# Row maxima of the second query chunk: the causal mask added by VectorE inside the maximum, in place of a masking product on TensorE

## The chip, the cores and the metric

The kernel runs on one core of a Trainium2 chip. The metric is the device time of one execution in microseconds (us). The kernel before took 1107.32 us (median of 3 runs, 1106.44 to 1109.43).

## The reference

Four sequences of 1024 rows of 256 numbers go through a linear attention (layer norm, three projections, no softmax), and then through a block with causal softmax attention (16 query heads, 4 key/value heads, 16 numbers a head) and a mixture of experts (8 experts, the top 2 for each row). What the change touches is the softmax:

```
scores = jnp.einsum('bqhd,bkhd->bhqk', q, k) * scale
causal = jnp.tril(jnp.ones((S, S), dtype=bool))
scores = jnp.where(causal[None, None], scores, jnp.finfo(scores.dtype).min)
probs = jax.nn.softmax(scores, axis=-1)
attn = jnp.einsum('bhqk,bkhd->bqhd', probs, v).reshape(B, S, NH * HD)
x = x + jnp.einsum('bso,ho->bsh', attn, wo)
```

The softmax subtracts each query row's maximum over the keys it may see. That maximum is what is computed in another way.

## The kernel before

All work is cut into steps with names ("max", "score", "pv", "wo", ...). A planner, `plan()`, runs before the program is built: it holds a price for each step on each engine (`work_of`, L159 to L183, and the table above it), plays all steps against each other, and writes out a fixed order for each engine. The program then follows these orders, and semaphores carry every dependency. So a changed price or a changed dependency in the planner moves instructions that the change does not name.

Per batch there are a projection part, four head groups (one key/value head and its four query heads) of attention, and a closing part. The head groups of one batch overlap with the projections of the next, and later with expert blocks. After the last head group only expert blocks are left.

A head group works in two query chunks of 512 rows (`r` is 0 or 1). For each chunk three things happen:

- **Row maxima** ("max", L1902 to L1921 on TensorE, L1715 to L1724 on VectorE). TensorE lays query rows on the PSUM partitions and keys on the columns: 128 query rows of a head against all keys that they may see. In the second chunk (r = 1) one unit is one head and one block jj of 128 query rows: a product over the first 512 keys (L1914) into one bank, and one over the w = 128, 256, 384 or 512 keys of the own chunk (L1919) into the next bank. The last 128 of these columns lie on the diagonal: there a third product (L1920, identity times a triangle of -1e38) adds the mask. VectorE then takes the maximum over all 512 + w columns (L1724) into one column of `mx`. There are 16 such units in a second chunk, and 16 head groups, so 256 units. In the first chunk the units take 2 or 4 heads at once (L1917, L1919, L1920; 96 VectorE instructions in all).
- The maxima are transposed (L1925), split and negated (L1731, L1733), and sent by SyncE into two extra rows of the stacked queries (L984), so that the score product itself subtracts them.
- **Scores and values** ("score" L1932, exponential on ScalarE L1267, mask of the probabilities on GpSimd L1121, "pv" L1946). The result leaves through ScalarE (L1274) into `heads_out`, and SyncE "packs" it into `attnT` (L995, L998).

A "max" unit of the second chunk takes two of the seven PSUM banks that all steps share. They come free when L1724 has finished. The planner also holds back a TensorE step whose follower on VectorE would have more than 1.7 us of work ahead of it.

At the end of a batch, "wo" multiplies `attnT` with the output weights (L1953), VectorE adds the residual (L1746), and "square_sum" on ScalarE (L1220) squares each row for the next norm; the squares themselves go to a scratch tile `squares`, only their sum is used. Each waits for the one before it, as both write that tile. The pack of the next batch waits until the last "wo" has read `attnT` (L996).

Where the planner sees TensorE idle it puts in dummy products ("warm", L1826).

Of the kernel before, what the change touches and what calls it, by code (L numbers as in the profile page):

```python
# [9 lines left out]
BF16 = mybir.dt.bfloat16  # L10
I32 = mybir.dt.int32
U32 = mybir.dt.uint32
ALU = mybir.AluOpType
ACT = mybir.ActivationFunctionType
AX = mybir.AxisListType

P = 128
NBATCH, SEQ, D = 4, 1024, 256
KD = D // P
TPB = SEQ // P  # L20
# [138 lines left out]
def work_of(step):  # L159
    stage, *at = step  # L160
    if stage == "gram":
        took = ("PE", 0.865 * TPB / gram_steps(at[0]))
        return (took, ("ACT", 0.49)) if at[1] == gram_steps(at[0]) - 1 else (took,)
    if stage == "split":
        b, c, u, i = at
        return ((("DVE", 0.6) if not b else ("POOL", 1.22), ("ACT", 0.53), ("POOL", 1.13), ("ACT", 0.53), ("DVE", 0.6) if not b else ("POOL", 1.13))[i],)
    if stage == "max":
        b, g, r, u = at
        jj, h0, nh, pitch, w = max_units(r)[u]
        columns = CH + w if r else nh * w  # L170
        return ("PE", (columns + P * nh) / 2400 + 0.01), ("DVE", 0.07 + columns / 960)
    if stage in ("score", "pv"):
        b, g, r, kt = at[:4]
        w = CH - max(kt * P - r * CH, 0)
        if stage == "score":
            n = heads_in(r, kt)[0]
            return ("PE", n * w / 2400 + 0.01), ("ACT", 0.06 + n * w / 1200)
        last = kt == KEYS[r][-1]
        return (("PE", 0.23 + w / 600), ("ACT", 0.49)) if last else (("PE", 0.23 + w / 600),)
    if stage == "up":  # L180
        took = 1.72 if at[0] < STAGED else 1.82
        return (("PE", took), ("DVE", 0.6)) if at[1] else (("PE", took), ("ACT", 0.49), ("DVE", 0.6))
    return WORK_OF[stage]  # L183
# [15 lines left out]
def plan():  # L199
# [39 lines left out]
    def needs(step):  # L239
# [79 lines left out]
            packed = [("pack", *chunk_at(m - 2))] if at[3] == last_kt[at[2]] and m > 1 else []  # L319
            return [scored, ("v", b, 1)] + before + packed  # L320
        if stage == "pack":
            closed = [("wo", b - 1, TPB - 1)] if b else []
            i = b * KD + at[1] // 2 - 1
            return [("pv", *at, last_kt[at[2]])] + closed + [("recip_store", i // KD, i % KD)] * (i >= 0)
        if stage == "recip":
# [342 lines left out]
def mega_kernel(nc, x, wtheta, wphi, wgT, ln1, ln2, wqkvT, wo, woT, gateT, w13T, w2T,  # L668
                rope_q, rope_k, eye, tri, ids, out):
    with ExitStack() as ctx:  # L670
# [5 lines left out]
        def sb(name, shape, dt=F32):  # L676
            return ctx.enter_context(nc.sbuf_tensor(name, shape, dt))[:]
# [9 lines left out]
        def grid(view, a):  # L687
            return view.rearrange("p (a b) -> p a b", a=a)
# [44 lines left out]
        ln2_s = sb("ln2_s", [P, KD])  # L733
        ident = sb("ident", [P, P])
        identb = sb("identb", [P, P], BF16)
        causal = sb("causal", [P, P], BF16)
        before = sb("before", [P, P], BF16)
        onesb = sb("onesb", [P, P], BF16)

        st = sb("st", [P, 2 * TPB * 6]).rearrange("p (s t c) -> p s t c", s=2, t=TPB)  # L740
        mv = sb("mv", [P, 2 * TPB * 2]).rearrange("p (s t c) -> p s t c", s=2, t=TPB)
        sumsq = sb("sumsq", [P, TPB])
        squares = sb("squares", [P, D], BF16)
        rt = sb("rt", [P, 3 * 6 * TPB]).rearrange("p (s a t) -> p s a t", s=3, a=6)

        scales, shifts = (sb(n, [P, NBATCH * 2 * TPB]).rearrange("p (b a t) -> p b a t", b=NBATCH, a=2) for n in ("scales", "shifts"))
# [44 lines left out]
        route_mem = sb("route_mem", [P, sum(route_sizes)])  # L791
        assert max(NB) * (NE - 1) <= 4 * n8
        routing = [carve(route_mem, route_sizes)] * len(GROUPS)

        def hot(gi):
            return routing[gi][4].bitcast(BF16)[:, 0:len(GROUPS[gi]) * TPB * NE]
# [108 lines left out]
        def _(e):  # L905
# [37 lines left out]
            for step in orders["SP"]:  # L943
# [42 lines left out]
                elif stage == "pack":  # L986
# [6 lines left out]
                    q.wait_ge(*slot("pack", 2, m - 2, NPACK))  # L993
                    landed(q, "recips_store", 2, b * KD + g // 2)
                    e.dma_start(sums[part * 32:(part + 1) * 32, :], heads_out[m % 2][HD:P:32, :]).then_inc(sem[f"pack{m % 2}"], 16)  # L995
                    q.wait_ge("wo_mm", TPB * b)  # L996
                    for hh in range(GRP):
                        e.dma_start(attnT[row + hh * HD:row + (hh + 1) * HD, k, r * CH:(r + 1) * CH], heads_out[m % 2][32 * hh:32 * hh + HD, :]  # L998
                                    ).then_inc(sem[f"pack{m % 2}"], 16)
# [171 lines left out]
        def _(e):  # L1171
            q = Queue(e, sem)
            for step in orders["ACT"]:
# [39 lines left out]
                elif stage == "square_sum":  # L1213
# [2 lines left out]

                    q.wait_ge("norm3", NORM3_STEPS * (b - 1) + 1)

                    q.wait_ge("square_sum", nth[step] - 1)
                    e.activation(squares, hrow[:, j, 0:D], ACT.Square, accum_out=sumsq[:, j:j + 1]).then_inc(sem["square_sum"], 1)  # L1220
                elif stage == "xnT":
                    b, c = at
                    q.wait_ge("xnT_mm", nth[step])
# [85 lines left out]
        def _(e):  # L1309
# [322 lines left out]
            for step in orders["DVE"]:  # L1632
                stage, *at = step
                if stage == "prepare":
# [3 lines left out]
                    e.tensor_scalar(causal, tri_in[:, 0:P], MASKED, None, ALU.mult).then_inc(sem["const"], 1)  # L1638
                    e.tensor_copy(before, tri_in[:, P:2 * P]).then_inc(sem["const"], 1)
                    e.memset(onesb, 1.0).then_inc(sem["const"], 1)  # L1640

                    e.memset(pv_bank, 0.0).then_inc(sem["const"], 1)
                    q.wait_ge("load_wqkv", 32)
# [71 lines left out]
                elif stage == "max":  # L1715
# [1 line left out]
                    jj, h0, nh, pitch, w = max_units(r)[u]  # L1717
                    to = mx[:, r, :].rearrange("p (h j) -> p h j", h=GRP)[:, h0:h0 + nh, jj]
                    took = turn[step][0]
                    took = took[:, 0:CH + w].unsqueeze(1) if r else took[:, 0:nh * pitch].rearrange("p (h k) -> p h k", h=nh)[:, :, 0:w]  # L1720
                    q.wait_ge("max_mm", nth[step])

                    q.wait_ge("maxT_mm", chunk(b, g, r) - 1)
                    e.tensor_reduce(to, took, AX.X, ALU.max).then_inc(sem["max"], 1)  # L1724
                elif stage == "maxT":
                    b, g, r = at
                    m, bk = chunk(b, g, r), turn[step][0]
# [87 lines left out]
        def _(e):  # L1815
            q = Queue(e, sem)
            offset = {}
            for step in orders["PE"]:
# [83 lines left out]
                elif stage == "max":  # L1902
# [8 lines left out]
                    for c in range(nh):  # L1911
                        rows_of = s[0:STACK, r, h0 + c, jj * P:(jj + 1) * P]
                        if r:
                            e.matmul(bk[:, 0:CH], rows_of, s[0:STACK, 0, GRP, :], start=True, stop=True)  # L1914
                        to = bk[:, CH:CH + w] if r else bk[:, c * pitch:c * pitch + w]
                        if w == P and not r:
                            m = e.matmul(to, rows_of, s[0:STACK, r, GRP, 0:w], start=False, stop=c == nh - 1)  # L1917
                        else:
                            e.matmul(to, rows_of, s[0:STACK, r, GRP, 0:w], start=True, stop=False)  # L1919
                            m = e.matmul(to[:, w - P:w], identb, causal, start=False, stop=True)  # L1920
# [126 lines left out]
```

## Time and profile before

| | |
|---|---|
| median of 3 runs | 1107.32 us |
| profiled execution, its own time | 1107.03 us |
| its span, first to last instruction | 1105.3 us |
| TensorE busy | 1063.3 us, 96% |
| VectorE busy | 742.3 us, 67% |
| ScalarE busy | 569.6 us, 52% |
| mean granted clock of TensorE | 0.992 |

A matmul's row covers its way through the array, so rows of matmuls overlap, and 96% busy does not mean that the array takes in columns 96% of the time: what one product costs is the distance from its start to the start of the next. The chain of waits is followed back from the last instruction, at each step to what released it; an engine's share of it says where the time of the run was decided.

### The profile page before, as it was taken

How to read it: one execution, taken by the hardware profiler on the slowest of the kernel's cores; microseconds unless marked ns; L12 is line 12 of the kernel's file. 1: busy time of each engine (PE TensorE's matmuls, PEld its weight loads, DVE VectorE, ACT ScalarE, POOL GpSimd, SP SyncE). 2: the span in 40 equal slices, each digit the busy share in tenths (PEclk: the TensorE clock that was granted, in tenths of full speed). 3: DMA queues.
4: the chain of work that ended last, by engine and by line, in shares of the span. 5: the costliest groups of instructions: out<-in, count | busy, mean ns of one | idle time of the engine just before them, and what ended most of it. 6: DMA issues, size and time to landing. Idle time of an engine off the chain costs nothing.

```text
span 1105.3 us, 20176 instructions
## 1 busy us (share of the span) xinstructions
PE 1063.3 (96%) x6972; PEld 660.7 (60%) x6972; DVE 742.3 (67%) x1530; ACT 569.6 (52%) x1106; POOL 407.8 (37%) x476
## 2 busy tenths in 40 slices
PE   7999999999998999899899999999999999999997
PEld 6766454564444333343344444446668999999996
DVE  4699997677677777669977689624484555555552
ACT  3564557646666788657466665663332222222220
POOL 1020413715532143331244532455547633333332
PEclk9999999999999899899999999999999999999999
DMA  6335121322225466542253340223344433222221
GB/s 189 122 101 153 38 79 57 94 73 82 85 75 149 152 194 209 150 142 79 66 138 96 86 139 25 52 68 84 96 92 105 97 49 49 46 45 45 47 42 11
DMA packets 85989, 102.32 MB, mean 93 GB/s; under 512 B 17121, under 2 KB 73569, under 8 KB 85889
## 3 DMA queue, kind: packets, MB, share of 16 engines
q1 hardware_dynamic: 71584, 81.39, 25.5%
q0 software_dynamic: 14304, 19.63, 9.5%
q8 instruction: 58, 0.95, 0.4%
q14 instruction: 43, 0.34, 0.1%
HBM read 56.15 MB, written 41.01 MB: 88 GB/s over the span
## 4 chain that ended last, share of the span: by engine, by line
PE 70%; DVE 20%; issue 3%; ACT 3%; DMA 2%; POOL 1%; SPq 1%; POOLq 0%; DVEq 0%
PE psum L1986 15%; PE psum L2002 11%; DVE mx L1724 10%; PE psum L1946 9%; PE psum L1978 7%; PE psum L1932 7%; PE psum L1919 3%; PE psum L1914 3%; PE psum L1953 3%; PE psum L1900 3%; ACT probs_mem L1267 2%; PE psum L1966 1%; PE psum L1845 1%; PE psum L1920 1%; PE psum L1993 1%
## 5 line engine op out<-in xcount | busy, mean ns | idle before, releaser
L1724 DVE TENSOR_REDUCE mx<-psum 128x1 f32<-128x640 f32 (+6 forms) x352 | 347.4, 1023 | 70.7 <-PE psum L1920 67.4
L1267 ACT ACTIVATE probs_mem<-psum 128x512 f32<-128x512 f32 (+1 forms) x608 | 308.1, 585 | 167.6 <-PE psum L1932 166.4
L1121 POOL TENSOR_SCALAR_AFFINE_SELECT probs_mem<-probs_mem 128x512 f32<-128x512 f32 x128 | 82.7, 647 | 304.7 <-ACT probs_mem L1267 304.5
L1166 POOL DMA_INDIRECT out<-yout,labels x71 | 112.0, 1577 | 208.7 <-DVE yout L1802 140.7
L1932 PE MATMUL psum<-stack_mem 98*128 98x512 bf16 (+3 forms) x768 | 173.2, 329 | 7.9 <-DVE mx L1724 4.0
L1946 PE MATMUL psum<-probs_mem,v 128*17 128x512 f32 (+3 forms) x1536 | 161.9, 497 | 2.6 <-POOL probs_mem L1121 1.4
L1919 PE MATMUL psum<-stack_mem 96*128 96x256 bf16 (+3 forms) x448 | 126.0, 313 | 0.1
L1932 PEld LDWEIGHTS psum<-stack_mem 98*128 98x128 bf16 x768 | 64.1, 98 | 90.3 <-DVE mx L1724 25.9
L1914 PE MATMUL psum<-stack_mem 96*128 96x512 bf16 x256 | 98.3, 388 | 8.8 <-DVE mx L1724 7.1
L1978 PE MATMUL psum<-w_mem,blockT 128*128 x200 | 95.2, 598 | 2.2 <-issue 1.6
L1920 PE MATMUL psum<-causal,identb 128*128 128x128 bf16 x448 | 96.6, 221 | 0.0
L2002 PE MATMUL psum<-w_mem,gatedT 128*128 x384 | 91.4, 381 | 0.2 <-ACT probs_mem L1267 0.2
L1986 PE MATMUL psum<-blockT,probs_mem 128*128 128x128 f32 x736 | 89.6, 275 | 0.0
L1986 PE MATMUL psum<-blockT,stack_mem 128*128 128x128 f32 x736 | 89.5, 275 | 0.0
L1986 PEld LDWEIGHTS psum<-blockT,probs_mem 128*128 128x128 f32 x736 | 87.6, 192 | 1.2
L1986 PEld LDWEIGHTS psum<-blockT,stack_mem 128*128 128x128 f32 x736 | 87.5, 192 | 1.2
L1291 ACT ACTIVATE gated<-psum 128x512 f32<-128x512 f32 x48 | 28.7, 597 | 105.9 <-PE psum L1978 57.5
L2002 PEld LDWEIGHTS psum<-w_mem,gatedT 128*128 128x128 f32 x384 | 70.6, 190 | 16.6 <-issue 8.7
L1786 DVE COPY blockT<-psum 128x256 f32<-128x256 f32 x71 | 29.9, 421 | 74.2 <-PE psum L1966 74.2
L1151 POOL DMA_INDIRECT routed<-hrow,route_mem x64 | 63.6, 994 | 20.1 <-issue 12.1
L1914 PEld LDWEIGHTS psum<-stack_mem 96*128 96x128 bf16 x256 | 24.9, 97 | 69.6 <-DVE mx L1724 37.6
L1946 PEld LDWEIGHTS psum<-probs_mem,v 128*17 128x17 f32 x1536 | 26.5, 95 | 66.1 <-issue 44.0
(209 smaller groups left out, 1509.3 us busy)
## 6 DMA issues: line engine op xcount, KB each, us to landing
block<-routed SPq DMA_DIRECT2D x71, 129.0 KB, 2.1
w_mem<-in_w13T SPq DMA_DIRECT2D x16, 512.0 KB, 5.6
qk_parts<-w_mem SPq DMA_DIRECT2D x16, 384.0 KB, 2.5
stack_mem<-qk_parts SPq DMA_DIRECT2D x32, 192.0 KB, 3.3
w_mem<-in_x SPq DMA_DIRECT2D x8, 512.0 KB, 5.3
out<-w_mem SPq DMA_DIRECT2D x8, 512.0 KB, 3.8
x_late<-out SPq DMA_DIRECT2D x8, 512.0 KB, 4.9
stack_mem<-qk_parts SPq DMA_DIRECT2D x32, 128.0 KB, 2.8
```

The source lines that it names most:

```text
L1121: e.affine_select(pb[:, :, q0:q0 + P], pb[:, :, q0:q0 + P], [[0, GRP], [1, P]], ALU.is_ge, 0.0, base=0, channel_multiplier=-1).then_inc(se ...
L1166: e.indirect_dma_start(out_rows, bass.IndirectOffsetOnAxis(ap=labels[w % NLABEL].bitcast(I32)[:, 0:1], axis=0), youts[w % NYOUT], None, bo ...
L1267: e.activation(probs[m % 2][:, hh:hh + n, q0:CH], grid(turn[step][0][:, 0:n * (CH - q0)], n), ACT.Exp, scale=float(HD) ** -0.5).then_inc(s ...
L1724: e.tensor_reduce(to, took, AX.X, ALU.max).then_inc(sem["max"], 1)
L1914: e.matmul(bk[:, 0:CH], rows_of, s[0:STACK, 0, GRP, :], start=True, stop=True)
L1919: e.matmul(to, rows_of, s[0:STACK, r, GRP, 0:w], start=True, stop=False)
L1920: m = e.matmul(to[:, w - P:w], identb, causal, start=False, stop=True)
L1932: m = e.matmul(bk[:, i * (CH - q0):(i + 1) * (CH - q0)], s[0:STACK + NMAX, kt // TPR, GRP, kt % TPR * P:(kt % TPR + 1) * P], s[0:STACK + N ...
L1946: m = e.matmul(pv_bank[32 * hh:32 * hh + HD + 1, q0:CH], v1[:, b, kt, g, :], pb[:, hh, q0:CH], start=(kt == KEYS[r][0]), stop=(kt == KEYS[ ...
L1978: m = e.matmul(bk, blockT[w % 2][:, k], w13_s[:, k, bass.ds(offset[w] + half * FFN, FFN)], start=(k == 0), stop=(k == KD - 1))
L1986: m = e.matmul(bk[:, c * P:(c + 1) * P], slots[w % NSLOT][:, k, half * FFN + c * P:half * FFN + (c + 1) * P], blockT[w % 2][:, k], start=( ...
L2002: m = e.matmul(bk[:, 0:D], rowsT[:, k * P:(k + 1) * P], w2_mem[:, bass.ds(offset[w] + k * D, D)], start=(k == 0), stop=(k == KF - 1))
```

## The change

The second chunk's masking product goes, and the maximum on VectorE becomes an instruction with two inputs that adds the mask, writes the sum back over the scores in PSUM, and keeps the maximum. The mask comes from a new tile: 512 columns of zeros, and behind them the triangle that `causal` was. The 512 + w columns are read as two rows of n = (512 + w) / 2; the pattern over the mask tile starts its two rows 128 columns apart, so that the first falls on zeros alone and the second ends in the triangle. The first chunk keeps its masking products and its plain maxima.

Besides this: `squares` is given up and L1220 writes its squares into the part of `attnT` that the "wo" before it has read, without waiting for its forerunner; the pack of the next batch therefore waits for the last "square_sum" in place of the last "wo"; the planner's price of a "max" unit of the second chunk loses 128 columns on TensorE and stays as it was on VectorE; one memset is added at the start.

```diff
-        return ("PE", (columns + P * nh) / 2400 + 0.01), ("DVE", 0.07 + columns / 960)
+        return ("PE", (columns + P * nh * (not r)) / 2400 + 0.01), ("DVE", 0.07 + columns / 960)
...
-            closed = [("wo", b - 1, TPB - 1)] if b else []
+            closed = [("square_sum", b - 1, TPB - 1)] if b else []
...
-        causal = sb("causal", [P, P], BF16)
+        masking = sb("masking", [P, CH + P], BF16)
+        causal = masking[:, CH:]
...
-        squares = sb("squares", [P, D], BF16)
...
+        def masked(w):
+            n = (CH + w) // 2
+            return bass.AP(masking.tensor, masking.offset + CH - (n - P) - P, [masking.ap[0], [P, 2], [1, n]])
...
-                    q.wait_ge("wo_mm", TPB * b)
+                    q.wait_ge("square_sum", TPB * b)
...
-                    q.wait_ge("square_sum", nth[step] - 1)
-                    e.activation(squares, hrow[:, j, 0:D], ACT.Square, accum_out=sumsq[:, j:j + 1]).then_inc(sem["square_sum"], 1)
+                    e.activation(attnT.bitcast(BF16)[:, 0, j * D:(j + 1) * D], hrow[:, j, 0:D], ACT.Square, accum_out=sumsq[:, j:j + 1]).then_inc(sem["square_sum"], 1)
...
+                    e.memset(masking[:, 0:CH], 0.0).then_inc(sem["const"], 1)
...
-                    e.tensor_reduce(to, took, AX.X, ALU.max).then_inc(sem["max"], 1)
+                    if r:
+                        q.wait_ge("const", 6)
+                        keys = grid(turn[step][0][:, 0:CH + w], 2)
+                        e.tensor_tensor_reduce(keys, keys, masked(w), 1.0, -3e38, ALU.add, ALU.max, to).then_inc(sem["max"], 1)
+                    else:
+                        e.tensor_reduce(to, took, AX.X, ALU.max).then_inc(sem["max"], 1)
...
-                        if w == P and not r:
+                        if r:
+                            m = e.matmul(to, rows_of, s[0:STACK, r, GRP, 0:w], start=True, stop=True)
+                        elif w == P:
                             m = e.matmul(to, rows_of, s[0:STACK, r, GRP, 0:w], start=False, stop=c == nh - 1)
```

On TensorE, early in the second chunk of the first head group, the program before has three products for each unit (L1914 the first 512 keys, L1919 the own keys, L1920 the mask), with scores (L1932) and values (L1946) between:

```order
L1914 MATMUL psum<-stack_mem 128x512
L1919 MATMUL psum<-stack_mem 128x256
L1920 MATMUL psum<-causal,identb 128x128
L1932 MATMUL psum<-stack_mem 128x384
L1914 MATMUL psum<-stack_mem 128x512
L1919 MATMUL psum<-stack_mem 128x256
L1920 MATMUL psum<-causal,identb 128x128
L1932 MATMUL psum<-stack_mem 128x384 x2
L1946 MATMUL psum<-probs_mem,v 17x512 x4
```

and the changed one, at the same place (L1926 is the old L1914, L1929 the own keys, L1946 the scores, L1960 the values):

```order
L1926 MATMUL psum<-stack_mem 128x512
L1929 MATMUL psum<-stack_mem 128x256
L1946 MATMUL psum<-stack_mem 128x384 x2
L1926 MATMUL psum<-stack_mem 128x512
L1929 MATMUL psum<-stack_mem 128x256
L1946 MATMUL psum<-stack_mem 128x384
L1960 MATMUL psum<-probs_mem,v 17x512 x4
```

The masking product is gone, and a score product has changed place with a unit, since the planner's times have shifted. Such exchanges go through the rest of the order. TensorE issues 5042 matrix instructions and loads of offsets where it issued 5290: 256 masking products fewer, 8 dummy products more (59 in place of 51).

On VectorE, at the start of the second chunk of the head group that meets the close of the first batch, the order before has single maxima with the short steps of a reciprocal root between them:

```order
L1383 TENSOR_SCALAR rt<-sumsq 128x8
L1724 TENSOR_REDUCE mx<-psum 128x1
L1322 TENSOR_SCALAR rt<-rt 128x8
L1724 TENSOR_REDUCE mx<-psum 128x1
L1325 TENSOR_SCALAR rstd<-rt 128x8
```

The changed order there:

```order
L1734 ISA psum,mx<-psum,masking 128x640
L1734 ISA mx 128x1
L1389 TENSOR_SCALAR rt<-sumsq 128x8
L1734 ISA psum,mx<-psum,masking 128x640
L1734 ISA mx 128x1
L1328 TENSOR_SCALAR rt<-rt 128x8
L1734 ISA psum,mx<-psum,masking 128x640
L1734 ISA mx 128x1
L1331 TENSOR_SCALAR rstd<-rt 128x8
```

Each maximum has become two instructions: one that adds, writes back and keeps the maximum, and a second with no tensor input that writes one column of `mx`. There are 256 such pairs. The short steps have moved behind one maximum that stood after them.

On SyncE, where the first packs of the second batch follow the close of the first (L984 the maxima, L995 and L998 the pack, L1022 and L1039 stores and weight loads), the order before is:

```order
L1039 DMA w_mem<-in_w13T 128x1024
L995 DMA sums<-heads_out 32x1x64
L998 DMA attnT<-heads_out 16x512 x4
L1022 DMA out<-x_late 128x256
L995 DMA sums<-heads_out 32x1x64
L998 DMA attnT<-heads_out 16x512 x4
L984 DMA stack_mem<-mneg_parts 1x16x128 x2
```

and the changed one (L990 the maxima, L1001 and L1005 the pack, L1029 the store):

```order
L1029 DMA out<-x_late 128x256
L990 DMA stack_mem<-mneg_parts 1x16x128 x2
L1029 DMA out<-x_late 128x256
L1001 DMA sums<-heads_out 32x1x64
L1005 DMA attnT<-heads_out 16x512 x4
L1001 DMA sums<-heads_out 32x1x64
L1005 DMA attnT<-heads_out 16x512 x4
```

The maxima now go out ahead of the first pack, and not behind the second.

## Rows read from the trace of the kernel before

**Rows 1.** The page: busy time of each engine; all maxima, busy, mean ns | idle before, releaser.
```profile
PE 1063.3 (96%) x6972; PEld 660.7 (60%) x6972; DVE 742.3 (67%) x1530; ACT 569.6 (52%) x1106; POOL 407.8 (37%) x476
...
L1724 DVE TENSOR_REDUCE mx<-psum 128x1 f32<-128x640 f32 (+6 forms) x352 | 347.4, 1023 | 70.7 <-PE psum L1920 67.4
```
**Rows 2.** Busy time in three stretches; columns as the second line says.
```profile
core 0: us, PE busy (x) PEld busy (x) DVE busy (x) ACT busy (x) POOL busy (x), PEclk, DMA share, GB/s
0.00:70.00 70.00, 60.74 (x318) 48.66 (x318) 46.82 (x204) 33.04 (x66) 9.70 (x22) 1.00 0.48 142
70.00:705.00 635.00, 609.67 (x4100) 284.92 (x4099) 500.23 (x945) 406.34 (x832) 224.09 (x266) 0.99 0.36 106
705.00:1105.00 400.00, 392.89 (x2557) 327.09 (x2556) 195.27 (x382) 130.24 (x209) 174.02 (x189) 1.00 0.32 63
```
**Rows 3.** Chain of waits, 70 to 705 us, by line: shares of the stretch.
```profile
by line: DVE mx L1724 18.1%; PE psum L1946 13.4%; PE psum L1932 10.2%; PE psum L1919 5.9%; PE psum L1914 5.6%; issue 4.3%; PE psum L1900 4.1%; PE psum L1953 3.9%; ACT probs_mem L1267 3.0%; PE psum L1978 2.6%; PE psum L1920 2.2%; DMA block<-
```
**Rows 4.** The line L1724: its forms, who waited for it (us, times).
```profile
L1724 DVE TENSOR_REDUCE mx<-psum x352: 669/1006/1227, 75.9 to 702.8; 128x1 f32<-128x640 f32 x32, 128x1 f32<-128x768 f32 x32, 128x1 f32<-128x896 f32 x32, 128x1 f32<-128x1024 f32 x32
...
  PEld psum L1914: 39.3, 65
  PEld psum L1932: 25.9, 40
  PEld psum L1925: 8.4, 18
```
**Rows 5.** Groups by shape, VectorE: busy, mean ns | idle before, releaser.
```profile
L1724 DVE TENSOR_REDUCE mx<-psum 128x1 f32<-128x1024 f32 x64 | 75.7, 1218 | 19.0 <-PE psum L1920 18.7
L1724 DVE TENSOR_REDUCE mx<-psum 128x1 f32<-128x896 f32 x64 | 67.2, 1083 | 14.2 <-PE psum L1920 13.9
L1724 DVE TENSOR_REDUCE mx<-psum 128x1 f32<-128x768 f32 x64 | 59.8, 951 | 15.5 <-PE psum L1920 15.5
L1724 DVE TENSOR_REDUCE mx<-psum 128x1 f32<-128x640 f32 x64 | 50.0, 810 | 1.2 <-PE psum L1920 0.8
L1724 DVE TENSOR_REDUCE mx<-psum 128x4 f32<-128x512 f32 x16 | 11.0, 687 | 2.3 <-PE psum L1917 2.3
L1668 DVE TENSOR_TENSOR w_mem<-psum,w_mem 128x512 f32<-128x512 f32 x16 | 11.0, 686 | 9.1 <-PE psum L1867 9.0
```
**Rows 6.** TensorE in order of time: start us, us.
```profile
348.45 0.27 PE L1919 MATMUL psum<-stack_mem 96*128 96x256 bf16 x1
348.56 0.22 PE L1920 MATMUL psum<-causal,identb 128*128 128x128 bf16 x1
348.62 0.38 PE L1914 MATMUL psum<-stack_mem 96*128 96x512 bf16 x1
```
**Rows 7.** VectorE in order of time, short steps between maxima.
```profile
345.75 0.81 DVE L1724 TENSOR_REDUCE mx<-psum 128x1 f32<-128x640 f32 x1
346.48 0.15 DVE L1322 TENSOR_SCALAR rt<-rt 128x8 int32<-128x8 int32 x1
346.55 0.81 DVE L1724 TENSOR_REDUCE mx<-psum 128x1 f32<-128x640 f32 x1
```
**Rows 8.** ScalarE in order of time: a sum of squares and its second instruction.
```profile
339.60 0.42 ACT L1220 ACTIVATE squares<-hrow 128x256 bf16<-128x256 f32 x1 [1.00 <-DVE hrow L1746]
339.93 0.19 ACT L1220 ACTIVATION_READ_ACCUMULATOR squares<-hrow 128x1 f32 x1
340.02 1.13 ACT L1212 ACTIVATE w_mem<-w_mem,ln_s 128x1024 f32<-128x1024 f32 x1
```
**Rows 9.** The last square of the first batch, and the pack behind it on SyncE.
```profile
344.61 0.41 ACT L1220 ACTIVATE squares<-hrow 128x256 bf16<-128x256 f32 x1
344.92 0.19 ACT L1220 ACTIVATION_READ_ACCUMULATOR squares<-hrow 128x1 f32 x1
...
344.46 2.44 SPq L998 DMA_DIRECT2D attnT<-heads_out  x4
```
**Rows 10.** VectorE's write into PSUM at the start.
```profile
L1642 DVE MEMSET psum<- 128x512 f32 x1 | 0.5, 485 | 0.1
```

More of the change, by code:

```diff
@@ L1719, in _ @@
                     took = turn[step][0]
-                    took = took[:, 0:CH + w].unsqueeze(1) if r else took[:, 0:nh * pitch].rearrange("p (h k) -> p h k", h=nh)[:, :, 0:w]
+                    took = took[:, 0:nh * pitch].rearrange("p (h k) -> p h k", h=nh)[:, :, 0:w]
                     q.wait_ge("max_mm", nth[step])
                     q.wait_ge("maxT_mm", chunk(b, g, r) - 1)
-                    e.tensor_reduce(to, took, AX.X, ALU.max).then_inc(sem["max"], 1)
+                    if r:
[4 more added lines that the diff above has]
+                        e.tensor_reduce(to, took, AX.X, ALU.max).then_inc(sem["max"], 1)
                 elif stage == "maxT":
```

## The prediction

> **What bounds the kernel now.** I read the page first. TensorE is busy 96% of the span, VectorE 67%, ScalarE 52% [rows 1]; so TensorE is the first suspect, but a matmul's row covers its way through the array, and says little about idle time. Second, the three stretches [rows 2]. All 352 maxima run between 76 and 703 us [rows 4], so only the stretch of 70 to 705 us can be touched. There VectorE is busy 500.2 of 635 us, 79%, and TensorE 609.7; in the 400 us of expert blocks behind it VectorE has half its time free and nothing of the change runs. Third, the chain of waits inside the stretch [rows 3]. The reader is to see two owners. The maxima L1724 alone hold 18.1% of it, more than any line of TensorE; the TensorE lines that the row names hold 47.9% together. So neither engine bounds the stretch alone: where the ring of PSUM banks is full, TensorE waits for a maximum; elsewhere VectorE waits for TensorE. Fourth, who waits at L1724 [rows 4]: VectorE sat idle 67.4 us before it until L1920 was done [rows 1], and in the other direction TensorE's weight loads waited 39.3, 25.9 and 8.4 us for L1724, in 123 waits. The waits go both ways. A microsecond saved on TensorE and one added on VectorE both count in part, and the question is which part.
>
> **The change, part by part.**
>
> *Removed on TensorE.* 256 masking products. Their row says 0.22 us, but the next product starts 0.06 us later, and the 256 columns of L1919 before it took 0.11 us from start to start, so 128 columns are 0.055 us [rows 6]. The clock there is the full one, and its mean in the stretch is 0.99 [rows 2]. 256 x 0.055 = 14.1 us of the array's time. That is one end: TensorE bound everywhere. For the other I take the chain: L1920 has 2.2% of 635 us = 14.0 us of it [rows 3], over 448 products, of which 256 go (352 maxima, of which 96 are the first chunk's, and L1920 stands 192 times there): 14.0 x 256/448 = 8.0 us. I take 9 us, near the chain's figure, since some of the 4.3% that the chain calls issue lies before such products. The range keeps 8 and 14, and zero for the case that the planner fills the room badly.
>
> *The maximum with the addition.* The same number of columns, but two inputs, a write of every column back into PSUM, and another reduction. No row of before shows this instruction. Rows next to it: a plain maximum over 512 columns takes 687 ns, and a two-input addition with one input in PSUM that writes 512 columns takes 686 [rows 5]. So a second input and a full output cost nothing against a maximum. A write into PSUM of 512 columns takes 485 ns [rows 10], less than either. The per-column part is (1218 - 810) / 384 = 1.06 ns [rows 5]. I take the first instruction at the old duration. Bounds: 0 below (I see no way in which two inputs are quicker than one), and above, a second pass per column, which is a rival below.
>
> *Added on VectorE: a second instruction.* The changed order has, behind each of the 256, an instruction without tensor input that writes one column of `mx`. The nearest relatives are the short steps of the reciprocal root. They last 0.15 us, but between two maxima they cost less: the short step starts 0.73 us after the maximum's start, before its 0.81 are over, and the next maximum follows 0.07 us later [rows 7]. ScalarE has the very pair already: its second instruction lasts 0.19 us and the next one starts 0.09 us after it [rows 8]. So a price of 0.07 to 0.09 us, and I take 0.08. The lower bound is 0.07. The upper: if nothing overlaps, 0.15 for the second instruction, plus the 0.08 (0.81 - 0.73) by which the maximum's end is now hidden, 0.23 us. At 0.08 it is 256 x 0.08 = 20.5 us of VectorE's time, which goes to 520.7 us. What of it is on the path? L1724 has 18.1% of 635 = 114.9 us of the chain, and 347.4 us of busy time [rows 1]: 33%. 20.5 x 0.33 = 6.8 us. The signal that frees the two banks comes with the second instruction, and is later by the same step, which this share already holds.
>
> The Trainium skill (VectorE: DVE Perf Modes, section Two Vector instructions with no wait between them) says that an operation which also writes its accumulator out is two instructions; the order of the changed program agrees.
>
> *The planner.* Its TensorE price for a unit falls by 128 columns, its VectorE price is not raised for the second instruction. It therefore believes VectorE 256 x 0.08 us quicker than I do, and holds TensorE back too late. The orders exchange score products and units throughout, and put 8 dummy products more. I cannot price that from rows; I take 0 with 4 us either way.
>
> *The squares.* The wait for the forerunner goes: the sixth square of the batch starts at 339.60 us and the eighth at 344.61 [rows 8, 9], 2.5 us apart each, so nothing was waiting there. The pack of the next batch now waits for the last square. In before it issued at 344.46 us, and the last square and its sum end at 344.92 + 0.19 = 345.11 [rows 9]: 0.65 us later, on SyncE, with the next maxima's transfer and the stack loads queued behind it. The changed order puts one transfer of maxima ahead of this pack, which takes what hurts most out of the queue. I cost it at 0, at most 0.7 for each of three batches. The added memset of 512 columns (485 ns, [rows 10]) falls in the first 70 us, where VectorE is free a third of the time [rows 2]: 0, or 0.5 if that cover is not there.
>
> **The sum.** -9 + 6.8 = -2.2 us. The profiled execution took 1107.03 us, so 1104.8 us; it stands 0.3 us under the median of the runs, which I let pass. Taking the balance the other way round: the change breaks even where the pair costs 9 / (256 x 0.33) = 0.107 us more than the single maximum.
>
> **The rivals.**
>
> *TensorE decides nearly everywhere.* For: it is at 96%, and what VectorE loses falls into its own idle time (70.7 us before L1724, [rows 1]). Then 14.1 us are gained and the short price of 0.07 is charged at half its share: 256 x 0.07 x 0.17 = 3 us. -11 us, 1096 us. Against: 123 waits of weight loads for L1724.
>
> *The pair does not overlap, and VectorE becomes the bound: slower.* Each unit costs 0.23 us more, VectorE is busy 500.2 + 58.9 = 559 us of the stretch, 88%. At today's share 58.9 x 0.33 = 19.5 us, less 8 us from TensorE: +11.5, 1118.5 us. Decisive is the distance from one maximum's start to the next's in an unbroken run: above 0.107 us over today's the change loses. For it: the second instruction needs what the first leaves behind, and may well wait for its end. Against: the ScalarE pair overlaps [rows 8].
> The Trainium skill (VectorE: DVE Perf Modes, The DRAIN you can't avoid) speaks for this one: the next operation does not start until the pipeline is empty. The trace agrees only in part, since a short step starts 0.08 us before the maximum's row ends [rows 7].
>
> *Half rate.* If the addition, the write back and the running maximum need two cycles a column, the second chunk's units (75.7 + 67.2 + 59.8 + 50.0 = 252.7 us, [rows 5]) cost their per-column part once more (1.06 ns by the 832 columns of their mean by 256 = 226 us) on VectorE, which then has 726 us of work in a stretch of 635. At least +91 us, 1198 us. For it only that no row shows such an instruction; against it the two-input additions at full rate.
>
> *It does nothing visible.* The freed array time goes into dummy products (0.055 x 4 a product on 8 more is under 2 us, so hardly) or into waits elsewhere: 1107.
>
> **How the numbers follow.** About 0.3% (3.3 us) is what can be told from no change here. The forecast's case, -2.2 with 4 to 5 either way, gets 0.50 (its own range is 1099 to 1110); of that 0.18 lie below 1104.0, 0.22 within, 0.10 above 1110.6. TensorE decides: 0.20, faster. No overlap: 0.22, slower. Half rate: 0.04. Nothing visible: 0.04. So faster 0.38, within 0.3% 0.26, slower 0.36. The range takes in the first rival with 3 us of the planner's and the second in its price: 1093 to 1119.
>
> **What would show it.** In the changed profile: L1926 to L1929 follow each other without a third product and TensorE's chain share for units falls by about 8 us; the first instruction of the pair lasts 0.81, 0.95, 1.08 and 1.22 us for the four widths; the second starts before the first has ended, and the next maximum comes 0.08 us behind; VectorE busy in the stretch near 520 us; waits of TensorE for the maxima longer than 74 us (39.3 + 25.9 + 8.4) by some 7. It is wrong if the pair's distance grows by more than 0.107 us, if the first instruction is longer than the old one by over 30 ns, or if the stretch of the experts, unchanged, moves by more than 2 us.

## The result and the profile after

The changed kernel takes 1103.74 us (median of 8 runs, 1100.93 to 1105.52), the kernel before in the same comparison 1109.53 (8 runs): the ratio is 0.995, with a 95% interval of 0.9933 to 0.9966, or 5.5 us less. The prediction was 1104.8 us with a range of 1093 to 1119. Part of this nearness is luck: it forecast 2.2 us less than 1107.03, and the kernel before took 1109.5 in this comparison, so a change of 5.5 in place of 2.2 still ended near the forecast time.

The page of the changed kernel, busy time of each engine, and the groups of the maxima (L1734 is the pair of the second chunk, L1736 the plain maximum of the first) and of their products (L1926, L1929):

```profile
PE 1052.8 (96%) x6732; PEld 643.1 (58%) x6732; DVE 751.1 (68%) x1787; ACT 570.3 (52%) x1106; POOL 406.9 (37%) x476
...
L1734 DVE CUSTOM_DVE_ANT_1 psum<-psum,masking 128x640 f32<-128x640 f32 (+3 forms) x256 | 256.7, 1042 | 36.5 <-PE psum L1929 34.5
...
L1736 DVE TENSOR_REDUCE mx<-psum 128x4 f32<-128x512 f32 (+2 forms) x96 | 96.9, 1040 | 19.0 <-PE psum L1934 15.1
L1926 PE MATMUL psum<-stack_mem 96*128 96x512 bf16 x256 | 94.3, 384 | 10.1 <-DVE mx L1734 6.7
...
L1929 PE MATMUL psum<-stack_mem 96*128 96x128 bf16 (+3 forms) x256 | 76.4, 298 | 0.0
```

Against [rows 1] VectorE has gained 8.8 us of busy time and TensorE lost 10.5. The chain of waits between 70 and 700 us, by line, answers to [rows 3]:

```profile
by line: DVE psum L1734 16.0%; PE psum L1960 12.7%; PE psum L1946 9.9%; DVE mx L1736 5.1%; PE psum L1926 4.7%; issue 4.5%; PE psum L1912 4.1%; PE psum L1967 3.9%; PE psum L1992 2.8%; PE psum L1933 2.6%; PE psum L1929 2.5%; ACT probs_mem L12
```

The maxima held 18.1% and hold 21.1% (16.0 + 5.1); the masking product of the second chunk is gone from it. The line of the pair (first and last start of its two instructions, then who waited for it, us and times) answers to [rows 4]. L1926 is the old L1914, L1946 the old L1932, L1939 the old L1925:

```profile
L1734 DVE CUSTOM_DVE_ANT_1 psum<-psum,masking x256: 794/1038/1267, 90.0 to 696.2; 128x640 f32<-128x640 f32 x32, 128x768 f32<-128x768 f32 x32, 128x896 f32<-128x896 f32 x32, 128x1024 f32<-128x1024 f32 x32
L1734 DVE DVE_READ_ACCUMULATOR2_ANT mx<- x256: 82/139/143, 90.7 to 697.4; 128x1 f32 x128
...
  PEld psum L1926: 41.0, 77
  PEld psum L1946: 28.8, 45
...
  PEld psum L1939: 5.9, 12
```

In [rows 4] the first chunk's maxima are in the same line. Here they have their own, L1736, and who waited for it has to be added:

```profile
  PEld psum L1946: 3.5, 6
  PEld psum L1939: 1.7, 4
```

The three groups of weight loads so wait 41.0, 28.8 + 3.5 = 32.3 and 5.9 + 1.7 = 7.6 us for the maxima, 80.9 together, where they waited 73.6.

The last maximum started at 702.8 us, and the last second instruction now starts at 697.4: what lies behind (402.5 us before, 403.0 after, spans 1105.3 and 1100.4) has not changed. The whole gain is in the attention stretch, where the instructions of the change are. What each piece of the change costs there is read from the order of time. VectorE in an unbroken run of maxima, of after:

```profile
123.48 0.81 DVE L1734 CUSTOM_DVE_ANT_1 psum<-psum,masking 128x640 f32<-128x640 f32 x1
124.22 0.13 DVE L1734 DVE_READ_ACCUMULATOR2_ANT mx<- 128x1 f32 x1
124.22 0.85 DVE L1734 CUSTOM_DVE_ANT_1 psum<-psum,masking 128x640 f32<-128x640 f32 x1
125.00 0.13 DVE L1734 DVE_READ_ACCUMULATOR2_ANT mx<- 128x1 f32 x1
125.00 0.85 DVE L1734 CUSTOM_DVE_ANT_1 psum<-psum,masking 128x640 f32<-128x640 f32 x1
```

and of before at the same place:

```profile
126.86 0.81 DVE L1724 TENSOR_REDUCE mx<-psum 128x1 f32<-128x640 f32 x1
127.59 0.94 DVE L1724 TENSOR_REDUCE mx<-psum 128x1 f32<-128x768 f32 x1
128.45 0.94 DVE L1724 TENSOR_REDUCE mx<-psum 128x1 f32<-128x768 f32 x1
```

A plain maximum over 640 columns is followed after 0.73 us, a pair behind another pair after 0.78. So the pair costs 0.05 us more. The first pair of the run, with no pair before it, is followed after 0.74. From there on each second instruction starts in the same moment as the next maximum, and that maximum's row is 0.85 us long and not 0.81. Where a short step stands behind it, it costs less still; the place of [rows 7] in after:

```profile
343.19 0.83 DVE L1734 CUSTOM_DVE_ANT_1 psum<-psum,masking 128x640 f32<-128x640 f32 x1
343.93 0.14 DVE L1734 DVE_READ_ACCUMULATOR2_ANT mx<- 128x1 f32 x1
343.93 0.17 DVE L1328 TENSOR_SCALAR rt<-rt 128x8 int32<-128x8 int32 x1
344.01 0.83 DVE L1734 CUSTOM_DVE_ANT_1 psum<-psum,masking 128x640 f32<-128x640 f32 x1
```

From maximum to maximum 0.82 us, where it was 0.80 with the short step alone: the second instruction and the short step start together, and the next maximum does not lengthen. On TensorE the products follow each other as [rows 6] promised, 0.11 us after the 256 columns of the own keys:

```profile
345.18 0.27 PE L1929 MATMUL psum<-stack_mem 96*128 96x256 bf16 x1
345.29 0.38 PE L1926 MATMUL psum<-stack_mem 96*128 96x512 bf16 x1
```

### The profile page after: what moved, and what is told of

It reads as the page before. It is cut to its first block, busy times and chain, and to the rows that moved or that the text cites. A ratio compares the mean times of both kernels' runs of the same rounds, so it can differ in the third digit from the quotient of the medians.

```text
span 1100.4 us, 19928 instructions
## 1 busy us (share of the span) xinstructions
PE 1052.8 (96%) x6732; PEld 643.1 (58%) x6732; DVE 751.1 (68%) x1787; ACT 570.3 (52%) x1106; POOL 406.9 (37%) x476
## 4 chain that ended last, share of the span: by engine, by line
PE 67%; DVE 22%; issue 3%; ACT 2%; DMA 2%; SPq 1%; POOL 1%; another core or an unknown queue 0%; DVEq 0%; POOLq 0%; ACTq 0%
PE psum L2000 15%; PE psum L2016 10%; DVE psum L1734 9%; PE psum L1960 8%; PE psum L1992 7%; PE psum L1946 6%; DVE mx L1736 3%; PE psum L1967 3%; PE psum L1912 3%; PE psum L1926 3%; PE psum L1933 2%; PE psum L1929 1%; ACT probs_mem L1273 1%; PE psum L1980 1%; PE psum L1857 1%
## 5 line engine op out<-in xcount | busy, mean ns | idle before, releaser
L1734 DVE CUSTOM_DVE_ANT_1 psum<-psum,masking 128x640 f32<-128x640 f32 (+3 forms) x256 | 256.7, 1042 | 36.5 <-PE psum L1929 34.5
L1946 PE MATMUL psum<-stack_mem 98*128 98x512 bf16 (+3 forms) x768 | 174.6, 330 | 8.7 <-DVE mx L1734 5.2
L1960 PE MATMUL psum<-probs_mem,v 128*17 128x512 f32 (+3 forms) x1536 | 161.0, 496 | 3.8 <-POOL probs_mem L1128 2.7
L1946 PEld LDWEIGHTS psum<-stack_mem 98*128 98x128 bf16 x768 | 65.9, 98 | 107.9 <-DVE mx L1734 28.8
L1736 DVE TENSOR_REDUCE mx<-psum 128x4 f32<-128x512 f32 (+2 forms) x96 | 96.9, 1040 | 19.0 <-PE psum L1934 15.1
L1926 PE MATMUL psum<-stack_mem 96*128 96x512 bf16 x256 | 94.3, 384 | 10.1 <-DVE mx L1734 6.7
L1929 PE MATMUL psum<-stack_mem 96*128 96x128 bf16 (+3 forms) x256 | 76.4, 298 | 0.0
L1926 PEld LDWEIGHTS psum<-stack_mem 96*128 96x128 bf16 x256 | 24.7, 97 | 78.4 <-DVE mx L1734 41.0
L1960 PEld LDWEIGHTS psum<-probs_mem,v 128*17 128x17 f32 x1536 | 26.8, 95 | 72.6 <-issue 43.6
```

Of the source, the lines that this page charges most:

```text
L1734: e.tensor_tensor_reduce(keys, keys, masked(w), 1.0, -3e38, ALU.add, ALU.max, to).then_inc(sem["max"], 1)
L1929: m = e.matmul(to, rows_of, s[0:STACK, r, GRP, 0:w], start=True, stop=True)
L1946: m = e.matmul(bk[:, i * (CH - q0):(i + 1) * (CH - q0)], s[0:STACK + NMAX, kt // TPR, GRP, kt % TPR * P:(kt % TPR + 1) * P], s[0:STACK + N ...
L1960: m = e.matmul(pv_bank[32 * hh:32 * hh + HD + 1, q0:CH], v1[:, b, kt, g, :], pb[:, hh, q0:CH], start=(kt == KEYS[r][0]), stop=(kt == KEYS[ ...
```

## The experiments

All ratios are against the kernel before in runs on the same chip, with the 95% interval. Where a difference is given in us, it is the ratio's distance from 1 times 1108; 0.001 of an interval is 1.1 us. Theory A is the prediction's: the missing products gain, the pair loses, each by the share of its engine on the path. Theory B: the order that the planner writes anew is what brought the gain.

**The masking products alone are left out**, in the order of before. The mask is missing from the second chunk's maxima.

```diff
-                        if w == P and not r:
+                        if r:
+                            m = e.matmul(to, rows_of, s[0:STACK, r, GRP, 0:w], start=True, stop=True)
+                        elif w == P:
```

> The kernel before without the second chunk's 256 masking products, and nothing else: plain maxima, the planner's prices and so every order as before (the maximum then runs over keys behind the diagonal too, so the mask is left out of the second chunk's maxima). Theory A, both engines count in part: the 14.1 us of array time give 8 to 10 us, 0.991 to 0.993 of before. Theory B, the gain of the change came from the new order: 0 to -3 us. Theory C, TensorE decides nearly everywhere: -13 to -14 us, 0.988.

Measured: 1102.07 us, 0.9955 (0.9940 to 0.9969), -5.0 us. Below theory A's 8 to 10: of 14.1 us of array time 35% shows in the time. Who waited for the maxima in this kernel (its L1914, L1934 and L1927 are the L1914, L1932 and L1925 of [rows 4]):

```profile
  PEld psum L1914: 46.6, 73
  PEld psum L1934: 30.0, 46
  PEld psum L1927: 8.6, 18
```

That is 85.2 us where it was 73.6. TensorE comes earlier to products whose banks a maximum still holds, and waits 11.6 us longer for them.

**The pair alone**, the products kept, the orders of before, and the squares in attnT as in the change.

```diff
-                    e.tensor_reduce(to, took, AX.X, ALU.max).then_inc(sem["max"], 1)
+                    if r:
...
+                        e.tensor_tensor_reduce(keys, keys, masked(w), 1.0, -3e38, ALU.add, ALU.max, to).then_inc(sem["max"], 1)
+                    else:
+                        e.tensor_reduce(to, took, AX.X, ALU.max).then_inc(sem["max"], 1)
```

> The masking products stay and the addition with maximum comes on top, in the orders of before (the squares written into attnT, for room). The pair's starts stand 0.78, 0.92, 1.05, 1.18 us apart in an unbroken run where the plain maxima stood 0.73, 0.86, 1.00, 1.13: 0.05 each. Theory A: 256 x 0.05 x 0.33 = +4.2 us, or +1.3 us if a short step beside it hides most of the second instruction; 1.001 to 1.004. Theory C: under +1 us. The forecast's price of 0.08 would give +6.8 us.

Measured: 1112.06 us, 1.0044 (1.0030 to 1.0058), +4.9 us, a little over the top of theory A's. The squares of this kernel cost 0.4 by the run with the squares in the order of before, below (0 within its interval), so the pair costs some 4.4 us, give or take 2. Of 256 x 0.05 = 12.8 us on VectorE that is 34%. The 12.8 are an upper bound, since not every pair stands behind another one: VectorE's busy time in this kernel's profile is 752.7 us, against 742.3 in that of the squares alone, so 10.4 us, of which 4.4 is 42%.

**Both, and the squares, in the order of before**: the whole change, with the planner's price and dependency put back.

```diff
-        return ("PE", (columns + P * nh * (not r)) / 2400 + 0.01), ("DVE", 0.07 + columns / 960)
+        return ("PE", (columns + P * nh) / 2400 + 0.01), ("DVE", 0.07 + columns / 960)
...
-            closed = [("square_sum", b - 1, TPB - 1)] if b else []
+            closed = [("wo", b - 1, TPB - 1)] if b else []
```

> The whole change with the planner's old prices and dependencies, so that every engine runs the order of before, less the masking products and with the pair. Theory A: the sum of the two runs above, -9 + 4 = -5 us, 0.995, the same as the changed kernel. Theory B: 0. If it lands at -9 or better, the new order costs time.

Measured: 1107.11 us, 0.9997 (0.9984 to 1.0010). The parts add to -0.1 and the whole is -0.3: the exchange of a product against a second instruction is worth nothing that can be told here. This is theory B's number, though the parts themselves are not zero, as B would have it. Who waited for the pair in this kernel (us, times):

```profile
  PEld psum L1926: 51.6, 84
  PEld psum L1946: 29.8, 48
  PE psum L1926: 10.6, 27
```

With the same instructions but the dummy products, TensorE's weight loads wait 51.6 and 29.8 us for the pair where the new order has 41.0 and 28.8. The profiled execution of this kernel was its slowest (1110.31 us, granted clock 0.987), and that of the changed kernel one of its faster ones (1102.14, 0.995), so this difference is larger than that of typical executions may be.

**The squares alone**, in planner and program, and **the squares in the order of before**. The first has the dependency of the pack in the planner too (the first pair of lines), the second only in the program.

```diff
-            closed = [("wo", b - 1, TPB - 1)] if b else []
+            closed = [("square_sum", b - 1, TPB - 1)] if b else []
...
-                    q.wait_ge("wo_mm", TPB * b)
+                    q.wait_ge("square_sum", TPB * b)
...
-                    q.wait_ge("square_sum", nth[step] - 1)
-                    e.activation(squares, hrow[:, j, 0:D], ACT.Square, accum_out=sumsq[:, j:j + 1]).then_inc(sem["square_sum"], 1)
+                    e.activation(attnT.bitcast(BF16)[:, 0, j * D:(j + 1) * D], hrow[:, j, 0:D], ACT.Square, accum_out=sumsq[:, j:j + 1]).then_inc(sem["square_sum"], 1)
```

> The kernel before with the squares in attnT and the pack of the next batch behind the last square, in planner and program, and nothing else. Theory A: 0, at most +0.7 us a batch by the wait, and up to 3 us either way by the order that the planner then writes. Theory B: some us faster.

> The squares in attnT, without their wait, and SyncE's pack behind the last square, but in the planner the old dependency, so in the order of before. If the 2.8 us of e4 came from the wait that is gone on ScalarE, they are here too: 0.9975. If they came from the new order, 0 to +1 us here. It also says how much of the +4.9 us of e2 belongs to the squares.

Measured: 1104.34 us, 0.9974 (0.9962 to 0.9987), -2.9 us, and in the order of before 1109.32 us, 1.0004 (0.9991 to 1.0018). The removed wait and the later pack cost and bring nothing that can be told; the dependency, by moving the order, brings 2.9 us.

**The planner's price alone**, on the kernel before, whose products stay.

```diff
-        return ("PE", (columns + P * nh) / 2400 + 0.01), ("DVE", 0.07 + columns / 960)
+        return ("PE", (columns + P * nh * (not r)) / 2400 + 0.01), ("DVE", 0.07 + columns / 960)
```

> The kernel before with only the planner's TensorE price of a second chunk's unit lowered by 128 columns, although the products stay: the order alone moves. The change is 5.5 us faster than before, the whole change in the old order is 0, the squares alone -2.8. If the two order effects add, this is -2.7 us, 0.9975. If the new order pays only together with the missing products, 0 or a loss.

Measured: 1104.94 us, 0.9965 (0.9951 to 0.9978), -3.9 us, with a price that is wrong for its instructions. The chain of this kernel from 70 to 700 us:

```profile
by line: PE psum L1946 16.3%; PE psum L1932 12.7%; DVE mx L1724 10.9%; PE psum L1919 7.1%; PE psum L1914 6.7%; PE psum L1900 4.1%; issue 4.0%; PE psum L1953 3.9%; PE psum L1978 3.7%; ACT probs_mem L1267 3.3%; PE psum L1920 2.6%; PE psum L18
```

The maxima hold 10.9% of it and held 18.1% [rows 3], with not one instruction of theirs changed. So an engine's share of the chain belongs to an order as much as to its work.

**No mask in the maxima, in the new order**: the first experiment with the change's squares, dependency and price.

> The second chunk's mask left out of the maxima (plain maxima, no pair), with the change's squares, dependency and TensorE price, so in the orders of the change. If the parts add: -5.0 (products gone) and -5.5 (order), 1107.1 - 10.5 = 1096.6 us; if the pair costs nothing once the order is the new one, the same as the changed kernel, 1101.6.

Measured: 1098.83 us, 0.9907 (0.9885 to 0.9928), -10.3 us: the -5.0 and the -5.5 add. The pair costs in the new order 4.8 us (-5.5 against -10.3, give or take 3) and in the old one 4.4, which cannot be told apart.

**Is the new order better, or a lucky one?** One planner constant moved on either kernel:

```diff
-AHEAD = {"DVE": 1.7, "ACT": 1.9}
+AHEAD = {"DVE": 1.8, "ACT": 1.9}
```

> The kernel before with one planner constant moved a little (how much VectorE work may be ahead of a TensorE step, 1.7 to 1.8 us), no instruction added or removed: what an arbitrary new order is worth. If the orders of e4 and e7 (-2.8 and -3.9 us) were a drawing of lots around a mean near before's, this lies within 4 us of before on either side; if before's order was a poor one of its kind, this too is 2 to 5 us faster.

> The changed kernel with the same constant moved in the same way. Lots: within 4 us of 1103.7 (ratio to before 0.991 to 0.999). If letting TensorE run farther ahead is what helps a VectorE that costs more than the planner believes, it is slower than the changed kernel, by 1 to 3 us.

Measured: before with it 1106.23 us, 0.9988 (0.9978 to 0.9999), -1.3 us; the changed kernel with it 1106.70 us, 0.9997 (0.9984 to 1.0009). The second number matters most: with a constant moved by 0.1 us the change is worth nothing, and against the kernel before with the same constant it is 1.0 us slower, which cannot be told from no difference. In the first one the maxima's share of the chain (70 to 705 us) is

```profile
by line: PE psum L1946 15.5%; PE psum L1932 12.0%; DVE mx L1724 11.8%; PE psum L1914 6.9%; PE psum L1919 6.7%; issue 4.2%; PE psum L1900 4.1%; PE psum L1953 3.8%; PE psum L1978 3.3%; ACT probs_mem L1267 3.0%; PE psum L1920 2.5%; PE psum L18
```

as low as in the run with the price alone, yet it gains a third of what that one gains. A lower share does not by itself say how much an order is better.

**The pair priced in the planner**, by its measured 0.05 us, and by 0.10 (`0.1 * r` in the same place).

```diff
-        return ("PE", (columns + P * nh * (not r)) / 2400 + 0.01), ("DVE", 0.07 + columns / 960)
+        return ("PE", (columns + P * nh * (not r)) / 2400 + 0.01), ("DVE", 0.07 + 0.05 * r + columns / 960)
```

> The changed kernel with the planner's VectorE price of a second chunk's unit raised by the 0.05 us that the pair costs in an unbroken run; everything else as in the change. If the planner loses by not knowing the pair (the forecast's worry), this gains 1 to 4 us on the changed kernel: 1100 to 1103. If what the new order brought was a lucky exchange and no better balance, it lands anywhere within 4 us of 1103.7.

> As e5 with 0.10 us in place of 0.05 for the pair in the planner. If e5's gain of 3.7 us over the change came from a price that fits, this gives it back in part (0.993 to 0.995). If it came from holding TensorE back more, it stays at 0.992 or better. If it was lots, anything from 0.990 to 0.998.

Measured: 1099.90 us, 0.9917 (0.9899 to 0.9935), -9.2 us; and with 0.10 1103.75 us, 0.9977 (0.9962 to 0.9992), -2.5 us. The price that fits is the best of the three (none: -5.5). That is what theory A expected of a planner that knows the pair; but the steps between neighbouring orders are as large as the effect (the two runs with the constant), so three points do not show that it is more than luck.

**The first batch left as before**, with products and plain maxima, and the pair priced elsewhere.

```diff
+PLAIN = 1
...
-        return ("PE", (columns + P * nh * (not r)) / 2400 + 0.01), ("DVE", 0.07 + columns / 960)
+        return ("PE", (columns + P * nh * (not r or b < PLAIN)) / 2400 + 0.01), ("DVE", 0.07 + 0.05 * (r and b >= PLAIN) + columns / 960)
...
-                    if r:
+                    if r and b >= PLAIN:
```

> The changed kernel with the pair's price known to the planner (as in e5), and in the first batch the masking products and plain maxima as in before: there the maxima hold 30 to 49% of the chain in the kernel before, so that array time is worth little and VectorE's much. 64 units get back 0.05 us each at a share near one half (-1.6 us) and give 64 x 0.055 us of array time back at a small one (+0.5): 1 us better than e5, 0.991, with some us of order either way.

Measured: 1097.18 us, 0.9912 (0.9896 to 0.9928). Against the 0.9917 of the pair priced by 0.05 no difference that can be told. Both beat the kernel before, and by the ratios of their two comparisons the changed one (0.9950) too.

## Why the prediction was right, and where it was not

The time, the direction and the likeliest case hold, but for a reason that the text did not give. Its sum was -9 + 6.8 with 0 for the order; the runs say -5.0 + 4.4, nothing together, with about -5 for the order. That the terms it had too large on either side cancelled, and that the order came out on the good side, is luck.

- *Removed on TensorE*, "I take 9 us, near the chain's figure": measured 5.0. This term was mis-sized, and lies below both figures between which it chose (8.0 and 14.1); only the zero kept for the range was below it. The array time itself, 0.055 us a product, was right. The chain gave L1920 8.0 us, and the chain tells where the time was decided, not what is left when a piece is taken out: the waits for the maxima grew by 11.6 us in the run without the products. The clock is a second part: that run had a lower granted clock than the kernel before, which by the estimate in the last section cost 1.8 us. At an equal clock the products would have given some 6.8 us, nearer to the chain's 8.0. How the missing 4 us are shared between the two was not tested by a run.
- *The maximum with the addition*, "at the old duration": right. 0.81, 0.95, 1.08 and 1.22 us stand in the stretch of 342 to 358 us; over the whole run the means are 22 to 31 ns longer than those of [rows 5] (836, 973, 1114 and 1246 ns), so one width passes the limit of 30 that the text set. Most of the excess is not the addition's: the first pair of an unbroken run reads 0.81 for 640 columns, as before, and those that start together with a second instruction 0.85.
- *The second instruction*, "I take 0.08": 0.05 in an unbroken run, 0.02 beside a short step, below the lower bound of 0.07. The bound was read off a short step of another kind, and was no bound for this one, which starts together with what follows and lengthens a following maximum by 0.04 us. So VectorE's busy time between 70 and 705 us went to 510.0 us and not to 520.7.
- *The share of 33%*: 4.4 of 12.8 us is 34%, and of the 10.4 us of busy time 42%. With the 2 us by which the 4.4 are uncertain (19% to 50% of 12.8), the chain's share of busy time agrees with the cost of lengthening the maxima; one run does not show more.
- *The planner*, "I take 0 with 4 us either way": this is the step that carried the result, a term put at 0. The dependency of the pack gives -2.9, the price -3.9, and the two together -5.2 (the whole change in its own order against the old: 0.9950 and 0.9997, with about 2 us either way). Its worry was that a planner that does not know the second instruction loses. With the pair at 0.05 us in its price the kernel is 3.7 us faster still, which fits the worry, but an order moved at random moves the time by as much.
- *The squares*: 0, as predicted, in the program; not in the planner.
- *The rivals*. "TensorE decides nearly everywhere" wanted 14.1 us from the products, and they gave 5.0. "The pair does not overlap" wanted 0.23 us a unit, against 0.05; its point of decision, 0.107, was worked out with the 9 us. With the measured 5.0 and 34% it lies at 5.0 / (256 x 0.34) = 0.057 us, and the pair with 0.05 sits just below it. "Half rate" fell with the durations. "It does nothing visible" is what the change does in the old order.

The waits of weight loads for the maxima were to grow by some 7 from 73.6 us: they are 80.9 in the new order, 7.3 more. In the old one, in its slowest execution, they are 51.6 + 32.2 + 9.5 = 93.3, with the first chunk's maxima counted in. So the forecast size of this sign came out in an order that the forecast had not priced, which is luck as well.

What stays open: why one order beats another by 3 to 5 us, beyond the part of the clock in the last section. The same waits fell from 73.6 to 54.1 us in the run with the price alone and to 60.9 in the one with the constant on the kernel before, and only the first gained much.

## What to carry to other kernels

Where a planner or scheduler writes the order, measure a change in the old order and in the new one: here the instructions exchanged were worth 0 and the order 5.2 us, and one constant moved by 6% took the gain away. What was lengthened here cost about its share of the chain; what was removed gave less than its share, since part of it came back as waits and part as a lower clock. When an instruction becomes a pair, give the planner the measured distance between two of them.

## What the runs showed that I had not expected

The second instruction of the pair and a following independent short step start in the same moment (343.93 us twice), and together cost 0.01 to 0.02 us more than the short step alone.

In the profiled execution of the kernel before, TensorE's granted clock fell to the lower level, 1.2 GHz, behind a stretch in which it waited for maxima. A long wait on TensorE there, in order of time:

```profile
359.49 0.39 PE L1914 MATMUL psum<-stack_mem 96*128 96x512 bf16 x1 [1.82 <-DVE mx L1724]
```

and the stretches around it (columns as in [rows 2]):

```profile
355.00:362.00 7.00, 4.21 (x25) 1.32 (x23) 6.04 (x20) 7.00 (x18) 0.63 (x1) 0.94 0.76 252
362.00:368.00 6.00, 6.00 (x27) 1.35 (x26) 2.45 (x2) 2.65 (x5) 0.63 (x1) 0.50 0.58 231
368.00:371.50 3.50, 3.43 (x32) 1.31 (x30) 2.17 (x2) 2.74 (x5) 0.00 (x0) 1.00 0.00 0
```

TensorE was busy 4.21 of 7 us, and then worked 6 us at 0.50. The kernel before has two stretches at the lower level between 70 and 705 us (from 361.1 and from 456.7 us), 13.7 us together, and the changed kernel two (from 378.5 and from 542.3 us), 6.8 us together. Over the span the clock is 0.992 before and 0.995 after in these two executions.

The mean clock of every execution of the changed kernel and of the experiments was recorded, so the clock's part can be estimated. Among eight runs of the changed kernel the four at 0.995 or above took 1100.9 to 1102.6 us and the four at 0.992 to 0.994 took 1104.9 to 1105.5. Over 204 executions, each against the mean of its own kernel, the time is 0.64 us (0.53 to 0.76) longer for each 0.001 that the clock is lower. This gives the clock's part of the differences, as an estimate:

| kernel | against before, us | mean clock (before: 0.9927 in 78 executions) | of it by the clock, us |
|---|---|---|---|
| products left out, old order | -5.0 | 0.9899 | +1.8 |
| whole change, old order | -0.3 | 0.9905 | +1.4 |
| whole change, its own order | -5.5 | 0.9942 | -1.0 |
| products left out, new order | -10.3 | 0.9947 | -1.3 |
| squares, planner and program | -2.9 | 0.9930 | -0.2 |
| price alone | -3.9 | 0.9954 | -1.7 |
| before, constant at 1.8 | -1.3 | 0.9964 | -2.4 |
| pair priced by 0.05 | -9.2 | 0.9922 | +0.4 |

So of the 5.2 us between the two orders of the whole change the clock would explain some 2.4, and of the 5.3 us between the two orders without the products some 3.1. It explains nothing of what the squares' dependency and the fitting price of the pair bring, and the constant on the kernel before raised the clock the most and gained little. By this estimate the clock is about half of what the new order brings, and not the whole. No run changed the clock alone, so this rests on executions of the same kernel that differ, and not on an experiment.
